# Six-attention megakernel on Trainium2: the score masks of three stages added in VectorE's row maxima

## The reference, cut to what matters

```python
scores = jnp.einsum('bhqd,bhkd->bhqk', Q, K) / sqrt(16)
scores = jnp.where(mask, scores, -jnp.inf)
attn   = jax.nn.softmax(scores, axis=-1)
out    = jnp.einsum('bhqk,bhkd->bhqd', attn, V)
```

## Time and profile before

| | kernel before |
|---|---|
| median of 3 runs | 1228.22 us |
| the profiled execution | 1226.54 us |
| its span | 1224.7 us |
| TensorE matmuls busy | 1182.9 us (97%), 14292 instructions |
| VectorE busy | 783.5 us (64%), 2123 instructions |
| ScalarE, GpSimd busy | 484.0 us (40%), 207.1 us (17%) |
| row maxima from PSUM (L1002) | 320 instructions, mean 682 ns |
| mask products of `scores` (L696) | 192 instructions |

### The profile page before, as it was taken

How to read it: one execution, slowest core, us unless ns; L and a number is a source line. 1 busy time by engine, 2 the same in 40 slices (tenths; PEclk the granted TensorE clock), 3 DMA queues, 4 the chain that set the end, 5 groups by cost and what they waited for, 6 DMA issues and landing times.

```text
span 1224.7 us, 35043 instructions
## 1 busy us (share of the span) xinstructions
PE 1182.9 (97%) x14292; PEld 956.4 (78%) x14292; DVE 783.5 (64%) x2123; ACT 484.0 (40%) x1126; POOL 207.1 (17%) x319
## 2 busy tenths in 40 slices
PE   5999999999999999999999999999999999999987
PEld 4877888877778888787788687888778778877866
DVE  4556577786986556555876856665785676467641
ACT  1343333322344363353344254434334435343533
POOL 0022122211111012111211121022022012112110
PEclk9999999998999999999999999999999999999998
DMA  7700001011202000001110100100011001001000
GB/s 248 295 2 2 2 3 44 2 44 44 88 2 71 6 14 6 6 9 49 45 56 6 44 13 16 35 18 13 6 44 56 6 17 45 1 7 44 11 6 10
DMA packets 22940, 43.98 MB, mean 36 GB/s; under 512 B 6528, under 2 KB 16896, under 8 KB 19712
## 3 DMA queue, kind: packets, MB, share of 16 engines
q1 hardware_dynamic: 21824, 40.30, 9.2%
q10 hardware_dynamic: 960, 1.44, 0.3%
HBM read 39.63 MB, written 2.10 MB: 34 GB/s over the span
## 4 chain that ended last, share of the span: by engine, by line
PE 76%; DVE 11%; issue 9%; POOL 2%; SPq 1%; DMA 0%; ACT 0%; POOLq 0%; DVEq 0%; ACTq 0%
PE bank L662 21%; PE bank L655 19%; PE bank L752 6%; PE bank L648 6%; PE bank L704 6%; PE bank L729 6%; DVE neg_max L1002 4%; PE bank L724 3%; PE bank L696 3%; PE bank L740 2%; DVE weight L1112 2%; PE bank L718 2%; DVE weight L1106 1%; PE bank L765 1%; POOL root L606 1%
## 5 line engine op out<-in xcount | busy, mean ns | idle before, releaser
L1002 DVE TENSOR_REDUCE neg_max<-bank 128x4 f32<-128x512 f32 x320 | 201.6, 682 | 51.4 <-PE bank L704 51.3
L606 POOL TENSOR_TENSOR root<-var_eps,halves 128x1 f32<-128x1 f32 x128 | 73.7, 577 | 832.4 <-DVE var_eps L1054 832.2
L875 ACT ACTIVATE exps_t<-bank 128x512 f32<-128x512 f32 x320 | 169.6, 609 | 90.9 <-PE bank L740 90.5
L662 PE MATMUL bank<-x_t,weights_A 128*128 128x128 f32 x1024 | 136.7, 282 | 2.8 <-ACT x_t L857 2.6
L662 PEld LDWEIGHTS bank<-x_t,weights_A 128*128 128x128 f32 x1024 | 125.7, 195 | 11.7 <-ACT x_t L857 4.9
L662 PE MATMUL bank<-x_t,weights_F 128*128 128x128 f32 x1024 | 125.8, 280 | 1.0 <-ACT x_t L857 0.9
L662 PEld LDWEIGHTS bank<-x_t,weights_F 128*128 128x128 f32 x1024 | 121.2, 195 | 4.6 <-ACT x_t L857 1.7
L655 PE MATMUL bank<-weights_F,exps_t 128*128 128x256 f32 x512 | 120.5, 382 | 0.0
L704 PE MATMUL bank<-k_eo,q_t 32*128 32x256 f32 x1536 | 111.0, 399 | 0.0
L752 PE MATMUL bank<-exps_t,v_one 128*32 128x128 f32 x3072 | 105.7, 276 | 2.1 <-ACT exps_t L875 0.8
L857 ACT COPY x_t<-bank 128x256 f32<-128x256 f32 x128 | 46.7, 381 | 153.2 <-PE bank L648 153.1
(11 more groups left out here) (104 smaller groups left out, 1734.0 us busy)
## 6 DMA issues: line engine op xcount, KB each, us to landing
weight<-in_fside SPq DMA_DIRECT2D x16, 1024.0 KB, 4.9
weights_A<-in_weights_A SPq DMA_DIRECT2D x4, 1028.0 KB, 18.2
weights_F<-in_weights_F SPq DMA_DIRECT2D x2, 2054.0 KB, 16.9
drop_raw<-in_drop SPq DMA_DIRECT2D x16, 256.0 KB, 5.3
x_hat<-in_x SPq DMA_DIRECT2D x16, 128.0 KB, 2.1
out<-x_sum SPq DMA_DIRECT2D x16, 128.0 KB, 1.7
ctx_t<-in_ctx_t SPq DMA_DIRECT2D x13, 128.0 KB, 4.9
rows_A<-in_rows_A SPq DMA_DIRECT2D x3, 512.0 KB, 19.0
```

The source lines that it names most:

```text
L606: nc.gpsimd.tensor_tensor(root[x][:], var_eps[x][:], halves[:, e:e + 1], ALU.pow).then_inc(done["root"], 1)
L662: mm = nc.tensor.matmul(dst[:, 128 * f:128 * f + 128], w[:, c, 128 * f:128 * f + 128], tokens_t[:, c, :], start=(c == 0), stop=(c == KC - 1))
L875: nc.scalar.activation(dst, score_bank(x, "ST", s, j)[:], ACT.Exp, scale=DH ** -0.5).then_inc(done["exp"], 1)
L1002: nc.vector.tensor_reduce(neg_max[x][:, j, :], heads, AX_X, ALU.max, negate=True).then_inc(done["max"], 1)
```

## The change

- `scores` keeps its mask product in A1 alone. In A0, A2 and A5 the score matmuls start the bank themselves, and the products of L696 are left out.
- `group_max` of A0, A2 and A5 gets four instructions in place of one, one for each head: `tensor_tensor_reduce` adds the 128 x 128 mask (bf16, SBUF) to the head's scores (fp32, PSUM), multiplies by -1, writes the result back over the scores in PSUM, and puts the minimum, which is the negative maximum, in one column of `neg_max`. Only the last of the four signals.
- `transposed_scores` keeps its mask products. It gets waits of its own for the mask, as VectorE does.
- All lists of beats and places are new; lanes, counts of beats and buffers are as before.

```diff
+PRELOADED = {"S": ("A1",), "ST": ("A0", "A2", "A5")}
+CAPPED = [s for s in ("A0", "A2", "A5") if s not in PRELOADED["ST"]]
+ADDED = [s for s in ("A0", "A2", "A5") if s not in PRELOADED["S"]]
...
 TENSOR = """
-12345112100100230011101340000101010100201000212202201301222222300001002033100023104033333111102113001113202042130432
+21354113100100200244315050001000000110112020011310103012120222220100100020130022301233011121113133301100100012324040
...
 def scores(x, s):
-                    masked = ATTN[s]["mask"] in (0, 1, 2, 3)
-                    if s == "A5":
+                    masked = s in PRELOADED["S"]
+                    if s == "A5" and masked:
                         pe.wait_ge(sxs_made, 1)
...
-                    if ATTN[s]["mask"] in (0, 1, 2):
+                    if masked and s != "A5":
                         pe.wait_ge(done["bias"], nth(x, "bias", "in"))
...
 def transposed_scores(x, s):
                     if masked:
+                        if s == "A5":
+                            pe.wait_ge(sxs_made, 1)
+                        else:
+                            pe.wait_ge(done["bias"], nth(x, "bias", "in"))
                         for j in range(GROUPS):
...
 def group_max(x, s, j):
+                    if s in ADDED:
+                        if s == "A5":
+                            dve.wait_ge(sxs_made, 1)
+                        else:
+                            dve.wait_ge(done["bias"], nth(x, "bias", "in"))
+                        for n in range(GH):
+
+                            ins = nc.vector.tensor_tensor_reduce(
+                                out=heads[:, n, :], in0=heads[:, n, :], in1=mask_bias(x, s), scale=-1.0,
+                                scalar=2.0 ** 126, op0=ALU.add, op1=ALU.min, accum_out=neg_max[x][:, j, n:n + 1])
+                        ins.then_inc(done["max"], 1)
+                        return
                     nc.vector.tensor_reduce(neg_max[x][:, j, :], heads, AX_X, ALU.max, negate=True
                                             ).then_inc(done["max"], 1)
```

More of the change, by code:

```diff
@@ new lines @@
+21311042121020002000022221200130230021233040444411113111414103144121222230302002000200033333013001523454303022222204
+22234123025300330000410231011004111155505540113441455443144455025050433334133332501004500001450441115411115155142551
+20555015331135223112222225034031450504442061266146641144411431624662666662466415226124622332242631361633333432556623
+13156625176666577366773422454457657657747757555744422656637752227672222333263333724743732356456747772776775375335727
+24626742856768878873386666888733888838878485646333355768355548734684444554734586468885887478884834335877834439577776
@@ new lines @@
+99587997888999989999799789459864746956695855665644465459664875865498856499959898988945956754464594a798878aa77958a577
+777a5a7a9aa9aaaa55556aa9a9a9576675a6859a9a96666867a67aaa5aa758575776aa5b7777bbabba7869996bbbb6bbbb6bb6ab9a99998b88a7
+6969a9aabab76b66688688886a798a67a96987bbbbbb76bba6678686caacc7accaaaa8aabbcaccc8bacccc88cc887c7bca8877779ab8cbcbbb87
+c7879b9b9978c999ccc7a88777d8dd8ccc9ccacaaac8998d88a8aaa88baac89dd9dddbdddcdddc9b9dcdbb9bbbbdbb8c8999bc9999b98ad9c88c
+dc88e9eebabeedc9ccc9e9beeeeceececc9ceea9caeebbcbbcbbbba9ebe99ea999b9aa9cebaa9ceee9eeaaeecddaee9ab9addddddd9b9bdeccdc
@@ L201 @@
+aec9faffaefafadefdfffadccccdffffadffaefaaaabfedebbbdfbbbdfabecbeacbafdcbdddcffffddddfffeddafffdadfeefeedbaafdbfbfbba
+deeeeeecffcebbbefbbcfbbebefdbdddbddddddffdbffdeffffcbbffbdfbdfdeeeefdedfdeeeddfddededdcececcccdcddfffddecfffffeffcef
+ddfdcedddedecdeefeedfecfcedecffffffffeccefefdceefdffccccffecdceecfdffeeeeffceffcfecfcfcdfeffffeeeee
 """
 VECTOR = """
-01234511211010101230000013400222202000012033300001012313010022111101024031132222202041044343403151201400000555352253
-33353112421204434051311431114444504333202000251545000000005001201400222545550523234141341235155023313121131311001114
@@ L205 @@
[L205 to L214, removed]
+01325411310100110000102234455001220202000012300003013121330111110102300012221100110021440422322424000001110220012330
@@ new lines @@
+03100212110132413333130104001010010000002220222002233200010530050434354325002200410151121211211111313340444410000501
+13433133150124143105050005043241242222252221111505551252244415111500533011233311111514522534444406226624266664623134
+33323363222246243343313166164236666636434444445452424353244645331735577565777223576746656722522223337533777266647437
+77727323565424574346676536575455653555555557747286888888833333388774444848678653876688688548737547474768338484557585
+85444394468995676699997946666666966888977559798559569888889996965794855664546469659577777777776777595558854a5aa79988
@@ new lines @@
+aaaa7a897a666a66aa9a5979755a797aaa9a7a6589799a97777788888888868685b868bbabbbb7ba6b6b6666a6a9ab6b89b9aab7a7bbb7b8b869
+9a97aa6968a78a6ab88877777876cccacccc8caab888b8caaacbbccb9ca98999c99999999b7bccbc7878c78cb9caa88aaaaaaaa7daadda88888c
+c8a99dddddbbbbcaa9c9bc9d98d99ddbd9999bb9888ccc9bbdbcddcccc8e9c9ee9addbdeeeeaeca99babbbebabbbbbcbeb99ba9ec99ebce9caac
+abeaaeeeebe9ce999ccccaceccbcbccababdbddcacecbddeece9fdaffaffffafaaaaafddfdbbbfbfbefededdaddbfdccaeaffaffbfbdbcccfcee
+ddeeffecdddffefdbbbbbbdadbdbeedddfdfdcfdededcefcdcdbecffffdfbcbddbfddeedeedeedeffeeeebedeffddddfdefffffdfeffedfdffdf
@@ L215 @@
+efefcddeeedddddefffcdeceeecfeffffcdfecffffdfdeccceccecdfeefffeeeeffeeffcffffcccefffcfdeeefe
 """
 SCALAR = """
[L217 to L224, removed]
+21354010100000001110121103120222210000203202133331111130001230411142022220000021302304444111111434122203333200000301
@@ new lines @@
+24530222242323053000001230111141555054441454554333331350000040441111151551245505135222220301505442464411116416266666
+46152622223426313331326315666627637454444765555777757666742272222333333723564777277753224678567666787868888383383384
+3555678534444454868858874833387777957898899999979894674444956666555564586598884899995894644a798777757aa55559aaaa9a5a
+9a765a66696867a6aa5aa5577a777b7b869999b9bbbbbbab98887a68a9ab666668a7869bbbbb6ba668caa7aacacacccb8cc888c8c7777a87bcbb
+879b9997c89cccc77d9caacaaa88888a89ddddddbcddc9dcbbbbbd8999b9998a9c88ebedc9ccecceeeeeceaebcbbbbb9e9999a9aaecbaa9eeeea
@@ L225 @@
+edddd9a9d9bdeccacccfefdefdadffffcffaaaaefadbbbbfbbeabdcddddfffffdafdafeedbeeafeffecebbbbfbbedbdddddfdbfffffcbbdfeedf
+eeeddddeddecccccdfffffecffdddddecdeeeefedeffffffecfdccccfdcedceeeefffeffcfcecffffeee
 """
 POOL = """
-00112000200301131224143302005523411435425024003531511440022255113332424004113535566442277666776353578876868887799868
-464699997776698889aa7755aa999aa886b6ababbccbba979aa7ccccbbccddaabbb88dddcdccbb99ddeeccaafefeeedddffffeeffdbdbeeeccff
-feeddffeeff
+00110020002101113003022122100043432332001115544441100335522244161652253336676762352435447778786644335558888797956544
@@ L230 @@
+66989a9a785977566aabba77a9968688abacbcbb7878c9c99dd88cbc9b9aaaecec99babbadeedddfefeaabbcccddffffeebbdddffddeeeccfffd
+eedffccffee
 """
 SYNC = """
-0010122123334455450123456666077718882999378aaa94abbb5ccc6bddd7cdeee8fff9eafbcdef
+000211223135443455012366604777158882699937aaa84bbb59ccc6addd7beee8cfffd9aebfcdfe
 """
 EXP_PLACES = """
-21222211222112122211211222111112112000100001200212112222212211112201010012012210110110111011110000111010101100101111
-111102221122
+22211211121211211222111122221022220110212222212221221122100222201112002022000002220102220000200022020121001102222220
@@ L238 @@
+000000201122
 """
 OUT_PLACES = """
-100001100101001000001110100101010001001111110101101001101110100011011100011100111000001000001111
+111010011000000010111001000001100001001111101101100011110101100101111100001110001111111011111111
 """
 PLACES = """
-76574475012357415216074123560472137421302356743232347610546217603542716343140276350271436720752071412713560413253535
-23746105273163014605171624031714134356203630714507126301707361645203716343031760752437024165741230647276426477426715
-30761253417526013252506052471603524740267134562076145324053712141424162045137620242162602534126243432324705163426021
@@ L247 @@
[L247 to L256, removed]
@@ L257 @@
-36216216750416265456252460317501024635065630530671246305712462426223642051705316421076541273617545656720317657246502
-14372146436262657142545214241036724135024671763567230142731560423125736143163512074513776251376313047236104253672467
-674102547753641554151111151
+76547745012345757160452320456571354720675453521406731754302626176125756712456437125230457360352147056350621756756575
+76756164302151765431360715234623057154201401014012010263752116402637405312760537612076341363630541206370414352610530
@@ new lines @@
+52613174056216126267346271304627156321076054736501427310516541272521036415072364154547125306205735410756236235410362
+57310436104326103547261613054107235060714021670545035435040352107073542127654320606172563416025237524603716504732713
+42617324617621753462120537146253207135247603154623706432132313565710452767315204031605341426731053127260547310525204
```

(11 more changed lines are left out.)

## The result

The changed kernel takes 1175.37 us in the median (1171.28 to 1176.73, 4 runs) beside 1228.17 us: ratio 0.9569, 95% interval 0.9542 to 0.9595, or -53 us. The forecast was 1199, its range began at 1181. The direction was right, the size was not: 53 us came off where 29 were expected.

What follows compares the result with a forecast made beforehand. The prediction took the middle of the kernel to be bound by a TensorE queue with few gaps. From 1226.5 us, -41.3 + 14.5 + 2 - 4 = -28.8 gave 1197.7, for a median of 1199 us, range 1181 to 1241.

Steps and rivals of the forecast that it cites:

- Products, -41.3 us: On TensorE, removing 192 mask products from scores, at 0.215 us each, takes 41.3 us off.
- The head, 0.30 us: On VectorE, each of 768 masked maxima costs 0.30 us (0.20 to 0.68), adding 115 us, to 898 us.
- VectorE's price, +14.5 us: VectorE at 75% busy raises TensorE's idle in the middle from 18.7 to 33 us: +14.5 us.
- The curve of idle time against busy share: TensorE's idle per 100 us against VectorE's busy share in profile windows: 1.5 at 72%, 3.4 at 80%, 7.3 near 98%.
- My point of no gain: The change makes the kernel slower above about 1060 us of VectorE work, or 0.51 us a head.
- The lists, -4 us: At the kernel's end, the new order fills gaps around sample 15's last work: -4 of 9.8 us idle.
- the 2 for two longer turns: The first and last stage turns have less work beside them to cover later maxima: 1 us each, +2.
- The signs: Profile marks if right: TensorE about 1145 us, VectorE about 900, idle about 33, head 0.27 to 0.35, m_parts waits some 10.
- The head is cheap: Rival, chance 0.17: at 0.20 us a head VectorE is 69% busy, TensorE's idle stays 1.5 to 1.6 in 100; 1183 us.
- The gaps move, they don't close: Rival, chance 0.12: maxima 2.4 us later in 48 stage turns, a third uncovered, bring back 38 us; 1222 us.
- VectorE becomes the bound: Rival, chance 0.21: in 48 turns of group_max, heads above 0.51 us make the kernel slower; 1243 us at 0.65.
- The note on the distance from scores to transpose in the new lists: Between scores and the maxima's transpose, the tightest A0 has 5.4 us of TensorE work, mostly covering VectorE's extra time.

Runs made afterwards that it cites:

- e1: The changed kernel with mask products back in scores of A0, A2 and A5 and one reduction a group again, keeping only the new lists: 1203.8 us.
- e3: The changed kernel with one plain reduction a group in A0, A2 and A5, so those maxima are of unmasked scores: 1161.4 us.
- e11: The changed kernel with one more constant-tile reduction ahead of each group's heads in A0 alone: 1204.5 us.
- e6: The changed kernel with one more constant-tile reduction ahead of each group's heads in A0, A2 and A5: 1278.1 us.
- e2: The changed kernel with the lists and places of the kernel before, so only the masks are moved: 1266.2 us.
- e8: The kernel before without mask products in scores of A0, A2, A5 (plain maxima), plus three constant-tile reductions a turn after the split of the maxima: 1244.6 us.
- e14: The kernel before without mask products in scores of A0, A2, A5 (plain maxima), plus three constant-tile reductions a turn ahead of the first maximum: 1287.2 us.
- e7: The changed kernel with two more constant-tile reductions ahead of each group's heads in A0, A2 and A5: 1412.8 us.

## Why the prediction missed

- **Products, -41.3 us.** Right for the lists that the change brings: 42.4 us (e1 to e3). In the old lists only 22.
- **The head, 0.30 us.** Measured 0.24 to 0.25, between the lower bound of 0.20 and my 0.30: VectorE at 853 us, not 898, and 69.5 us of work added, not 115. Two instructions a head, as the Trainium skill has it ("VectorE: DVE Perf Modes", "Two Vector instructions with no wait between them"), and the trace agrees, 768 reads of 138 ns; they were not held, and the lower of the two prices, 0.27, was nearer. (The upper one, 0.35 us, gives 937 us of VectorE, not the 914 written.)
- **VectorE's price, +14.5 us.** The measured 14.0 agrees by luck. I had put it on 115 us of work; the change adds 69.5, for which the windows near its 73% give 1.5 in 100, next to nothing more than before, and at 106 us (e11) the price is 43. Nor is it the idle that I read the curve from, which stayed at 18.2 us. The curve of idle time against busy share, read from windows of one pair of lists, does not carry over: the cost is a matter of which beats the lists let be late, and it rises steeply somewhere between 853 and 890 us. My point of no gain, 1060 us of VectorE, was near 911 (between e11 and e6, by their slope). Its own working has a slip too: the gain to lose was 41.3 + 4 - 2 = 43 us, not 39, which moves the point further up, away from the measured one.
- **The lists, -4 us: the step that failed.** The text costed the end at -4 and "a different permutation of everything" at nothing, left to the ends of the range. The new lists alone are worth -23 us (e1): about 9.4 at the end and 13 in the middle, which I had taken for a queue with few gaps because its windows idle just 18.7 us. The diff's largest part by far is those lists, and they got one of the smallest terms.
- **The sum.** For the masks it says -41.3 + 14.5 + 2 = -24.8, the 2 for two longer turns; measured in the new lists it is -28.4. For the lists it says -4, measured -23. Of the 23 us by which the sum fell short, 19 are the lists. That the whole of it, -28.8, is so near to the -28.4 of the masks alone is chance.
- **The signs.** 192 products gone, 768 instructions of each of two kinds and TensorE at 1135.5 us (some 1145) came true. A head at 0.25 us, VectorE at 853, the idle of 18 us instead of 33 and the waits for `m_parts`, which fell from 5.0 to 2.4 us where I had them grow to 10, did not.
- **Rivals.** "The head is cheap" came nearest with 1183 us, still 8 too many, and its idle of 1.5 to 1.6 in 100 is what the windows show; its price of nothing for VectorE is not what e3 shows, and it too gives the lists no more than -4. "The gaps move, they don't close" is what happens with the old lists: the wait named there (L804, now L813) grows from 5.0 to 11.1 us, and the whole is worse than priced, 61 us instead of 38, as the banks were not in it. The note on the distance from scores to transpose in the new lists fits what e2 and the change show, but it counts for slack the change needs, not for time gained. The loss that "VectorE becomes the bound" warns of starts far earlier than computed.

## What to carry to other kernels

When a change comes with a new hand- or search-made order, cost the order as an edit of its own: run the new order with the old work, and the old order with the new work. A kernel of in-order queues with 64% busy VectorE may have next to no slack (e8: half a us for each us, at the cheapest place tried), because what counts is how soon a bank is wanted again and how long after a product its consumer is due; extra work should go where the order leaves distance, and the order be made for it. And a TensorE that is 97% busy may still wait in many pieces too short to show: compare the busy time of kernels with the same matmuls, beside their granted clocks, and the engine shares of the chain.

## What was not expected of the hardware

- A masked maximum of 128 columns costs 0.25 us from start to start though its two instructions last 324 and 138 ns: the read of the accumulator hid wholly under the next head.
- Writing the scores back to PSUM and the read-out together seem to add about 0.05 us: 0.25 us against my estimate of 0.20 from instructions that only read PSUM. No run times the instruction without them.
- TensorE's granted clock was lower in most kernels in which it waited more: mean 0.994 after, 0.992 before, 0.977 in e2 and e14, 0.949 in e7 with two more reductions, where 5.1% of 1409.4 us, 72 us, are lost to the lower of its two levels, 1.2 GHz. The two do not go in step: e6, with 109 us not busy on its page, has 0.988, e2 with 87 has 0.977. The prices above hold the lost clock; that the late VectorE work brought it about is likely, but only read from these runs side by side.
